# A perceiver block on one core: the key and value projections drawn together, and a square root moved one place ahead

## The reference

```python
x = x + _L0_xattn_ref(_layernorm(x), ctx, ctx, ...)      # 1601 keys a sequence
x = x + _L0_attn_ref(_layernorm(x), ...)                 # selective scan
x = x + _L0_ffn_ref(_layernorm(x), W_fc, W_proj)         # squared ReLU, then 5 spike steps
x = x + _L1_xattn_ref(_layernorm(x), ctx, ctx, ...)      # 16 heads of 16, rotary, causal window
x = x + _L1_attn_ref(_layernorm(x), ...)                 # gated by distances of two phases
x = x + _L1_ffn_ref(_layernorm(x), ...)                  # 8 experts, top 2
```

```python
def proj(x, W, b):
    return (x @ W.T + b).reshape(x.shape[0], x.shape[1], H, Dh).transpose(0, 2, 1, 3)
q = apply_rope(proj(query, Wq, bq))
k = apply_rope(proj(key, Wk, bk))
v = proj(value, Wv, bv)
```

## Time and profile before

| | us |
|---|---|
| median of 3 runs | 699.85 |
| lowest and highest | 699.3 and 704.0 |
| the profiled execution | 699.3 |
| its span, first to last instruction | 697.6 |
| TensorE busy | 648.9 (93%) |
| VectorE busy | 475.6 (68%) |
| ScalarE busy | 367.1 (53%) |
| GpSimd busy | 221.5 (32%) |

### The profile page before, as it was taken

One profiled execution on the slowest core, in us unless ns is written; L12 is line 12 of the kernel. 1 busy time (PEld: TensorE's weight loads), 2 busy tenths in 40 slices (PEclk: granted clock), 3 DMA queues, 4 the chain that ended last, 5 costly groups with the idle time before them and its releaser, 6 DMA issues. The chain is left out here.

```text
span 697.6 us, 11272 instructions
## 1 busy us (share of the span) xinstructions
PE 648.9 (93%) x4226; PEld 450.2 (65%) x4226; DVE 475.6 (68%) x819; ACT 367.1 (53%) x675; POOL 221.5 (32%) x180
## 2 busy tenths in 40 slices
PE   3989999998997899899998999999999989999997
PEld 1445555564335556556665678888777766888897
DVE  5014333347858999998999853678787878777554
ACT  1222111124559898898998832434476455455442
POOL 2000000000005999998888400012573001222000
PEclk9999999999999999999999999999999999999999
DMA  8999999764631222222321000000200012120000
GB/s 313 386 359 417 419 420 419 315 245 143 160 94 31 91 100 110 93 93 90 112 100 61 1 0 1 17 0 1 50 2 3 1 62 76 47 61 1 31 0 31
DMA packets 31069, 86.45 MB, mean 124 GB/s; under 512 B 7900, under 2 KB 19576, under 8 KB 28840
## 3 DMA queue, kind: packets, MB, share of 16 engines
q1 hardware_dynamic: 30456, 85.28, 33.5%
q10 hardware_dynamic: 560, 0.46, 0.2%
HBM read 83.50 MB, written 1.11 MB: 121 GB/s over the span
## 5 line engine op out<-in xcount | busy, mean ns | idle before, releaser
L692 POOL TENSOR_TENSOR dbu<-du,bs 128x1024 f32<-128x1024 f32 x63 | 148.9, 2380 | 221.9 <-DVE du L899 209.3
L1031 PE MATMUL Y<-weighed,ident 128*128 128x512 f32 (+1 forms) x256 | 100.5, 513 | 0.0
L921 DVE TENSOR_TENSOR_SCAN w_in<-hS,dbu 128x1024 f32<-128x1024 f32 x42 | 95.2, 2277 | 0.0
L784 ACT ACTIVATE weighed<-T,CT 128x256 f32<-128x256 f32 x208 | 82.9, 474 | 16.7 <-PE T L1021 15.4
L773 ACT ACTIVATE hS<-delta,negA 128x504 f32<-128x504 f32 x128 | 83.2, 693 | 3.4 <-DVE xn L921 2.7
L1031 PEld LDWEIGHTS Y<-weighed,ident 128*128 128x128 f32 x256 | 43.5, 191 | 29.2 <-issue 29.2
L1021 PE MATMUL T<-ident,w_in 128*128 128x128 f32 x336 | 45.1, 276 | 10.3 <-ACT weighed L784 2.8
L1021 PEld LDWEIGHTS T<-ident,w_in 128*128 128x128 f32 x336 | 36.4, 140 | 26.4 <-DVE w_in L921 15.7
L921 DVE TENSOR_TENSOR_SCAN xn<-hS,dbu 128x1024 f32<-128x1024 f32 x22 | 50.2, 2280 | 3.2 <-issue 2.3
L265 PE MATMUL O<-cN,pT 128*64 128x256 f32 x384 | 46.7, 385 | 0.0
L359 ACT ACTIVATE prob<-S,nbias 128x1601 f32<-128x1601 f32 x8 | 12.8, 1596 | 63.0 <-DVE nbias L463 63.0
(11 more groups left out here) (419 smaller groups left out, 1344.5 us busy)
## 6 DMA issues: line engine op xcount, KB each, us to landing
cT<-in_ctxT SPq DMA_DIRECT2D x8, 3202.0 KB, 14.6
cN<-in_ctx SPq DMA_DIRECT2D x8, 3072.0 KB, 13.7
bs<-b_rows SPq DMA_DIRECT2D x32, 512.0 KB, 3.5
raw_w<-in_w SPq DMA_DIRECT2D x16, 256.0 KB, 2.8
w<-in_w SPq DMA_DIRECT2D x7, 256.0 KB, 8.2
vs<-vx SPq DMA_DIRECT2D x8, 136.0 KB, 2.3
x<-in_x SPq DMA_DIRECT2D x2, 512.0 KB, 5.9
cR<-in_ctx SPq DMA_DIRECT2D x1, 1024.0 KB, 31.9
```

Source lines behind the costliest of these rows:

```text
L692: e.tensor_tensor(dbu[s % NB][:, :, :], half(m.du, s // DS), row, ALU.mult).then_inc(s_bu, 1)
L784: i = e.activation(weighed[s % 2][:, q * Q:(q + 1) * Q], T[:, q * Q:(q + 1) * Q], ACT.Copy, scale=c_of(s, q))
L921: e.tensor_tensor_scan(S[s % NS], A[s % 2][:, :], dbu[s % NB][:, :, :].rearrange("p c n -> p (c n)"), 0.0, ALU.mult, ALU.add).then_inc(s_h, 1)
L1031: e.matmul(Y[:, w], k.ident[:, :], weighed[s % 2][:, w], start=False, stop=True, skip_group_check=True).then_inc(s_y, 1)
```

## The change

Three things change, all of them in the order of work.

1. The functions `project_keys` and `project_values` become one, `keys_and_values(p)`, which makes both waits first and then the eight matmuls. The pairs of quarters 0 and 1 move: both of quarter 0 now stand ahead of `project_value_bias`, and both of quarter 1 behind `turn_rotated(1, 1)`. In the last two pairs the wait for `("v", 2)` now stands ahead of the keys of quarter 3 as well.
2. `second_layer(3)` moves behind `turn_rotated(0, 1)` and `project(2)`. ScalarE's list follows: the copies stand where their transposes now do, and `move_turned2(3)` stands ahead of `root3(0)`.
3. In ScalarE's `step(5)`, `root(0)` takes the place of the 1-element square root, and leaves step 6.

VectorE, GpSimd and SyncE keep their order.

```diff
-        pe_steps = [("out", 2), ("t2", 0), ("t2", 1), *fc(0), ("t2", 2), ("out", 3), ("cb", 0), ("pr", 0), ("kp", 0),
+        pe_steps = [("out", 2), ("t2", 0), ("t2", 1), *fc(0), ("t2", 2), ("out", 3), ("cb", 0), ("pr", 0), ("kp", 0), ("vp", 0),
...
-            def project_keys(p):
+            def keys_and_values(p):
 
                 if p:
                     ve("k", p - 1)
-                else:
-                    ac("x2", 2)
-                for u in range(2):
...
-                done(j, "kp", p)
-
-            def project_values(p):
-
-                ac(*(("x2", 0), ("x3", 1), ("x3", 2), ("v", 2))[p])
...
-                done(j, "vp", p)
+                ac(*(("x2", 2), ("x3", 1), ("x3", 2), ("v", 2))[p])
+                for i, bank, name in ((1, O, "kp"), (2, T[0], "vp")):
+                    for u in range(2):
+                        t = 2 * p + u
+                        for c in range(KD):
+                            j = e.matmul(bank[:, u * D:(u + 1) * D], k.c0T[:, c, t * P:(t + 1) * P], k.w4[i][:, c, :],
+                                         start=c == 0, stop=c == 1)
+                    done(j, name, p)
...
             second_layer(0)
-            project_keys(0)
+            keys_and_values(0)
             project_value_bias()
             first_layer(1)
             turn_normed2(3)
-            project_values(0)
             second_layer(1)
             first_layer(2)
             turn_normed3(0)
-            project_keys(1)
             project(0)
             second_layer(2)
             project(1)
             first_layer(3)
             turn_rotated(0, 0)
             turn_normed3(1)
-            second_layer(3)
             turn_rotated(0, 1)
             project(2)
+            second_layer(3)
             turn_rotated(1, 0)
             scores(0, 0)
-            project_values(1)
             turn_rotated(1, 1)
+            keys_and_values(1)
             turn_normed3(2)
             step(0)
-            project_keys(2)
-            project_values(2)
-            project_keys(3)
-            project_values(3)
+            keys_and_values(2)
+            keys_and_values(3)
...
-                if i == 6:
-                    root(0)
...
-                if i in (1, 5):
+                if i == 1:
                     e.activation(warm[:, :], k.ident[:, 0:1], ACT.Sqrt)
+                if i == 5:
+                    root(0)
...
             move_y(0)
+            move_values(0)
             squares(1)
+            move_turned2(3)
             root3(0)
-            move_turned2(3)
-            move_values(0)
             move_y(1)
...
             move_normed3(1)
+            move_rotated(0, 1)
             root3(2)
             move_y(3)
-            move_rotated(0, 1)
             move_rotated(1, 0)
+            move_rotated(1, 1)
             move_values(1)
-            move_rotated(1, 1)
             move_normed3(2)
```

More of the change, by code:

```diff
@@ L1272, in ffn_and_heads @@
         nm = lambda q: [("ag3", q), ("ep3", q), ("rc3", q), ("xn3", q), ("cx", q)]
-        pe_steps = [("out", 2), ("t2", 0), ("t2", 1), *fc(0), ("t2", 2), ("out", 3), ("cb", 0), ("pr", 0), ("kp", 0),
-                    ("cb", 1), *fc(1), ("t2", 3), ("vp", 0), ("pr", 1), *fc(2), ("t3", 0), ("kp", 1), ("pr", 2), *fc(3), ("t3", 1),
-                    ("pr", 3), ("vp", 1), ("t3", 2), ("kp", 2), ("vp", 2), ("kp", 3), ("vp", 3), ("t3", 3),
+        pe_steps = [("out", 2), ("t2", 0), ("t2", 1), *fc(0), ("t2", 2), ("out", 3), ("cb", 0), ("pr", 0), ("kp", 0), ("vp", 0),
+                    ("cb", 1), *fc(1), ("t2", 3), ("pr", 1), *fc(2), ("t3", 0), ("pr", 2), *fc(3), ("t3", 1), ("pr", 3),
+                    ("kp", 1), ("vp", 1), ("t3", 2), ("kp", 2), ("vp", 2), ("kp", 3), ("vp", 3), ("t3", 3),
                     ("qp",), ("row",), ("qk", 0), ("sum",), ("reT",), ("sumsq",), ("qk", 1), ("pf", 0), ("pf", 1)]
-        ac_steps = [("r2", 1), ("x2", 0), ("x2", 1), ("r2", 2), *sq(0), ("x2", 2), ("cv", 0), ("r2", 3), ("y", 0),
-                    *sq(1), ("r3", 0), ("x2", 3), ("v", 0), ("y", 1), *sq(2), ("x3", 0), ("r3", 1), ("y", 2), *sq(3), ("x3", 1),
+        ac_steps = [("r2", 1), ("x2", 0), ("x2", 1), ("r2", 2), *sq(0), ("x2", 2), ("cv", 0), ("r2", 3), ("y", 0), ("v", 0),
+                    *sq(1), ("x2", 3), ("r3", 0), ("y", 1), *sq(2), ("x3", 0), ("r3", 1), ("y", 2), *sq(3), ("x3", 1),
                     ("r3", 2), ("y", 3), ("v", 1), ("x3", 2), ("v", 2), ("v", 3), ("r3", 3), ("x3", 3),
```

## The result

| | before | changed |
|---|---|---|
| median, us (19 runs each) | 701.13 | 704.48 |
| lowest and highest, us | 699.12 and 704.0 | 704.01 and 706.12 |
| profiled execution and its span, us | 699.3, 697.6 | 706.03, 704.3 |

The interval tells it all the same.

What follows compares the result with a forecast made beforehand. TensorE was taken to set the pace, busy 33.23 of 34.3 us in the heads. Terms 3.0 + 0.95 + 0.46 = 4.4 us on the 699.85 median gave a forecast of 704.2, bounds 702.7 to 705.2, 8-in-10 range 701.4 to 706.0.

Steps and rivals of the forecast that it cites:

- values of quarter 0 leave their place: Ahead of `second_layer(1)`: TensorE waits 1.08 us for the last square, 1.18 with the stop.
- keys of quarter 1 leave theirs: Ahead of `project(0)`: a wait of 1.62 us for `xT` plus 0.10, against 1.72 of projection gone; net 0.
- late second layer, up to tile 2: `second_layer(3)` starts 3.1 us later; VectorE's spike of quarter 3 and tile 2's turning move by 3.0.
- merged wait: `project_keys(3)` now waits 0.86 us for the copy of quarter 2's values, 0.95 with the stop; bounds 0.2 to 1.0.
- root: Early root delays the copy of turned probabilities, so transposes start 0.46 us later; bound from below -0.13.
- Is the 3.0 paid back?: Chain from the spike to tile 2 moves whole by 3.0 us; moved keys' 1.72 cost nothing, TensorE 0.5 or more early.
- Rival A: Chain to tile 2 gives way or later steps have room; 1 to 2 us come back, 701.4 to 703.0; chance 0.17.
- Rival B: No change or a little faster: stops at `second_layer(1)` and `project(0)` cost nothing; 699 to 701 us; chance 0.10.
- Rival C: A stop drops TensorE's clock to 1.2 GHz for one layer's block, 6.9 us more, 711; chance 0.04.
- any slice below 1.00: Sign in the changed kernel's profile: a slice's granted clock below 1.00 would mean Rival C.
- The experts' stage: Sign of being wrong: waits appearing in this stage, whose order is untouched, mean something outside the reckoning moved.
- The drain behind a table load: At the root: the skill page's drain of about 1.38 us would make the term about 0.85; the sum followed the trace.

Runs made afterwards that it cites:

- e5_keys1_back: Changed kernel with the keys of quarter 1 back between the first transposes into T[0] and the query projection of tile 0: stage 147.89 us, ratio 1.0052.
- b3_rotate4_early: Kernel before with keys of quarter 2 ahead of tile 2's turn, and VectorE's queries and rotation of tile 4 earlier: stage 142.65 us, ratio 0.9995.
- e6_three_back: Changed kernel with values of quarter 0 back, keys of quarter 3 without the values' wait, and root back in step 6: stage 145.90 us, ratio 1.0036.
- e1_late_wait: Changed kernel in which the keys of quarter 3 no longer wait for the copy of quarter 2's values: stage 147.03 us, ratio 1.0048.

## Why the prediction was right, point by point

The forecast was 704.2, the median is 704.48, inside 701.4 to 706.0. That is closer than the reasoning deserves. The difference that I forecast is 4.4 us; the stage shows 4.12, the ratio of whole executions 3.6. The total came out near because the three runs of before that I had stood 1.3 us below the median of nineteen: from that median the same 4.4 would have led to 705.5. The size of the change is right to 0.3 us; the last 1.3 us of agreement are luck.

| term | forecast | trace of the changed kernel | undone alone |
|---|---|---|---|
| values of quarter 0 leave their place | 1.18 | 452.85 - (443.33 + 6.91) - 1.43 = 1.18, at the next block | 1.16 |
| keys of quarter 1 leave theirs | 0 | 462.78 - 460.18 - 1.43 = 1.17, so 0 more | 0.0 |
| late second layer, up to tile 2 | 1.8 (to 3.0) | 496.99 - 492.56 - 1.43 = 3.00 | 1.84 with the keys, 0.89 without |
| merged wait | 0.95 | 0.93 at 503.22, 1.02 behind the stop, 516.16 - 510.89 - 1.43 - 3.00 = 0.84 from tile 4 on | 0.84 |
| root | 0.46 | 543.95 - 538.21 - 1.43 - 3.84 = 0.47, 0.28 from step 7 on | 0.29 |
| sum | 4.4 | 4.12 | 1.16 + 1.84 + 0.84 + 0.29 = 4.13 |

*Waits.* Each wait was where it had been put, and of its size: 1.07 ahead of `second_layer(1)` (445.83 - 443.33 - 1.43) for 1.08, and the second layer of quarter 3 late by 3.11 for 3.1. Laying steps from start to start against the releasing copy's end plus 0.06, and 0.10 for each stop, was good to a few hundredths, but for the merged wait, which was 0.07 longer than reckoned.

*What was over-sized.* The merged wait and the root, as the sum took them in full. Both are given back in part where TensorE next meets VectorE: at tile 4, where it had waited 0.31 before and no longer lists a wait (0.18 back), and in step 7 (0.19 back). I had named 0.2 and -0.13 as the lower bounds and taken values near the upper ends; the runs say 0.84 and 0.29.

*Is the 3.0 paid back?* Right: chain and distances are unchanged, and the moved keys are free at both places, shown by 1.95 of wait against 0.23. The margin at tile 2 was thinner than the 0.5 or more that I had: 0.23.

*Rival A* (the chain gives way, 1 to 2 us come back): of the 3.0 nothing came back, and 0.4 of the rest in later steps. Its range was also reckoned wrong: 1 to 2 us off 704.25 is 702.3 to 703.3, and not 701.4 to 703.0; so the lower end of my range, which was taken from it, stood 0.9 too low. *Rival B* (stops only an effect of modelled ends) falls: taking one stop away brought 1.16. *Rival C*: none of the stops in the stage let the clock fall. But the ground that I gave for this was thin. I held the row of 2.17 us near the start against it, and elsewhere in the program the clock did fall about stops of only 1.63 us, in some executions (last section). What kept it up in the stage no run here shows. The sign that I gave for it, any slice below 1.00, was a bad one: such slices are there, outside of the stage, and executions of the kernel before have a mean clock below 1.00 as well.

*The experts' stage.* I had named new waits there as a sign of being wrong. There are none: behind the second mark TensorE lists waits of 0.49, 0.68 and 0.64 in both traces, and 0.37 before against 0.38. The one of 1.22 for `pb` is missing in the changed kernel's profile, where the clock is below 1.00 up to that block; in `e5_keys1_back`, whose clock is level there, it is 1.22 again.

*The drain behind a table load.* The Trainium skill's page "ScalarE: Activation LUTs", section "What ACT_TABLE_LOAD costs", would have put this term, as an estimate, at about 0.85. With its load over at 542.12 and a drain of 1.38 the root could not have started before 543.50; it started at 543.11. In the kernel before, the load at 535.56 was over at 536.84, and its 1-element root ran right behind:

```profile
536.86 0.20 ACT L1765 ACTIVATE hwarm<-ident 128x1 f32<-128x1 f32 x1
```

The traces decide against the drain here.

## What to carry to other kernels

Work without dependencies that stands between two dependent steps is cover; before it is joined with its like elsewhere, lay the producer's end against the step that would follow bare, for every gap that it leaves. A wait that one engine loses is worth only what the next meeting of the engines leaves of it: look for the second engine's list between the two meetings before counting a filled wait as a gain. And when a few tenths are at stake, measure between two marks in the trace around the edit, since whole executions differ by more for reasons elsewhere.

## What the runs showed of the hardware

The granted clock of TensorE fell to the lower of its two levels, half speed, at three places in the changed kernel's profiled execution: around 46 us, around 226 us, and at the stop that ends the stage. The first two lie outside of the stage, and at the third TensorE is idle up to the second mark. Windows of that execution, columns as above, the third figure from the end being the clock:

```profile
42.00:46.00 4.00, 3.74 (x28) 3.15 (x28) 0.68 (x2) 0.60 (x1) 0.00 (x0) 1.00 0.97 412
46.00:50.00 4.00, 4.00 (x12) 1.19 (x14) 0.78 (x2) 0.00 (x0) 0.00 (x0) 0.57 0.99 412
...
226.00:230.00 4.00, 4.00 (x12) 2.68 (x12) 4.00 (x4) 2.38 (x5) 4.00 (x3) 0.50 0.06 24
415.00:568.00 153.00, 145.28 (x1427) 121.01 (x1425) 107.23 (x229) 70.30 (x119) 36.68 (x58) 1.00 0.04 9
568.00:570.00 2.00, 0.37 (x5) 0.16 (x4) 1.68 (x5) 1.09 (x3) 0.09 (x1) 0.65 0.00 0
570.00:574.00 4.00, 4.00 (x37) 3.52 (x38) 3.13 (x10) 1.55 (x3) 0.90 (x2) 0.50 0.70 174
```

and of the kernel before, around the same start of the next Block:

```profile
562.50:564.50 2.00, 0.37 (x6) 0.16 (x6) 1.68 (x5) 1.09 (x3) 0.14 (x1) 1.00 0.00 0
564.50:568.50 4.00, 2.98 (x40) 2.35 (x40) 3.08 (x10) 2.04 (x4) 0.85 (x2) 1.00 0.53 159
```

In both, TensorE stood still for 1.63 us at that boundary. In one execution the clock was 0.65 in the 2 us of the stop and 0.50 in the 4 behind it, in the other it stayed at 1.00. At the first place TensorE had stood 1.66, then done eight records of matmuls of 512 columns (from 39.04 to the next block at 42.58) and 16 of one column (1.84 us), and the clock fell behind these. At the second it had stood 1.57 and 1.50 shortly before (ahead of 222.09 and 224.69). At both places the kernel before did the same with the clock level. The stops of 0.91, 1.46 and 1.02 inside the changed stage never brought the clock down in any of the profiled executions. In two other versions the clock also fell somewhere between 600 and 697 us (0.98 over that stretch in `b3_rotate4_early` and `e6_three_back`). What decides between two equal executions, no run here shows.

The parts outside of the stage sort by these falls. The first mark comes at 420.10 to 420.65 in the four traces with a level clock ahead of it, at 420.90 to 421.56 in the four where it fell at the first place only, and at 421.34 to 422.09 in the six where it fell at both. From the second mark to the end it is 133.20 before, 133.17 and 133.25 in the two versions of the changed kernel whose clock was level there (`e1_late_wait`, `e5_keys1_back`), and 134.35 in the changed kernel's profile. So the 1.15 belongs to the clock of that one execution, and most of the 1.43 does, though that part also varies by half a microsecond at a level clock. Neither comes from the moved work.

What the clock costs is seen in whole executions sorted by their mean granted clock. Medians in us, number of executions in brackets, 83 of the kernel before and 30 of the changed:

| mean clock | before | changed |
|---|---|---|
| 1.000 | 699.25 (28) | none |
| 0.998 | 699.70 (3) | 704.16 (9) |
| 0.995 | 699.69 (3) | 704.46 (7) |
| 0.993 | 701.20 (26) | 704.68 (9) |
| 0.988 | 701.77 (21) | 705.67 (5) |

Two executions of before with 0.990 are left out. From a level clock to 0.988 the kernel before loses 2.5 us, six tenths of what the change costs. At equal clocks the change costs 3.5 to 4.8 us, around the 4.12 of the stage. That none of 30 executions of the changed kernel had a level clock, against a third of those before, I did not expect and can't explain. Two versions of the changed kernel do have such executions, four of 11 with the merged wait undone and two of 8 with the layer undone. Their medians, 702.34 and 702.51, lie 2.9 and 3.1 above the 699.41 of the five level ones of before beside which they ran; by the marks it should be 3.28 and 3.23. With the clock level, then, whole executions and the stage agree within 0.4 us.
